# An order and PSUM banks of its own for the first body of an attention loop written as lists of jobs

## The chip, the cores and the metric

One Trainium2 chip, one core of it. The metric is the device time of one execution in microseconds (us), as the median of several runs. The profile is of one further execution, recorded by the hardware profiler. TensorE is called PE, VectorE DVE, ScalarE ACT, GpSimd POOL, and SyncE, which issues the DMAs, SP.

## The reference

A transformer layer on x of 4 x 1024 x 256, all in float32. Layer norm, then attention with 16 heads: queries through a rank of 64, keys and values through a compressed rank of 64, a rotary part of 64 columns, a causal softmax over 1024 tokens, and the output product; then layer norm and a mixture of experts. Both are added to x. What matters here is the attention:

```python
qf = jnp.concatenate([q_nope, _rope(q_pe)], axis=-1)
kf = jnp.concatenate([k_nope, _rope(k_pe)], axis=-1)
scores = jnp.einsum('bhnd,bhmd->bhnm', qf, kf) * scale
scores = jnp.where(causal, scores, jnp.finfo(scores.dtype).min)
attn = jax.nn.softmax(scores, axis=-1)
out = jnp.einsum('bhnm,bhmd->bhnd', attn, v)
x = x + out.transpose(0, 2, 1, 3).reshape(b, n, HEADS * VDIM) @ Wout
```

The kernel has folded the key weights into the queries, so that a query and a key each have 128 numbers (64 of the latent, 64 rotary).

## The kernel before

Three stages follow each other: `attention_prepare` (keys, values and folded weights of all four batches), `attention`, and `ffn` (router and experts).

`attention` works on 32 **pairs of heads** (8 pairs for each of 4 batches). It is software pipelined: a **body** r holds jobs of several pairs, -1 <= r <= 32, and `age` (line 984) says which pair a job of body r belongs to. The jobs, with c the half of the tokens (512 queries), a the head in the pair:

- `Q(c,a)`: PE multiplies out 512 queries of a head, two matmuls of 512 columns. Then DVE does `ROT` (three instructions, lines 1333 and 1335), POOL `ADD` (line 1412), ACT `HIGH` (line 1262, the high part of a split of a float32 in two), POOL `LOW` (line 1419, the rest).
- `S(c,a,j)`: PE makes the scores of query block 4c + j (128 queries) against the (4c + j + 1) x 128 keys that the causal mask leaves: 128 to 512 columns for c = 0, 640 to 1024 for c = 1. Three products (high x high, high x low, low x high), each in one piece of at most 512 columns for c = 0 and in two for c = 1. DVE's `MAX` (line 1321) adds the mask and takes the row's maximum, ACT's `EXP` (line 1270) makes the exponentials in SBUF and their sum.
- `T(c,kb,a)`: PE transposes the 128 x 128 blocks of the exponentials for key block kb (line 1196), up to four, into one of three PSUM banks of their own; `OUT` copies them to SBUF, on ACT (line 1281) or DVE (line 1346). A `T` waits for all four `EXP` of its c and a, and for the `OUT` three transposing jobs back.
- `PV(c,first,n)`: PE multiplies them by the values; `O` on DVE, `OHIGH` on ACT, `OLOW` on POOL follow.
- `INV` (DVE), `REP` (POOL), `L` (PE) and `LOUT` (ACT) invert the sums of the softmax and repeat them; `Y` (PE) and `ACC` (DVE) add the output product to x.

The order of the work is written out by hand, in one list for each engine: `TENSOR`, `VECTOR`, `SCALAR`, `POOL` (lines 924 to 956), with `BANK` giving each `Q`, `S`, `L` and `Y` one of PSUM's banks 0 to 3 (two neighbours for the scores of c = 1). Each engine goes through its list in order, and waits at the head of it on semaphores. One list serves all bodies; a body leaves out the jobs whose pair doesn't exist. So body -1 has only `Q(0,1)` and `Q(0,0)`, the first half's queries of pair 0. Body 0 has all `Q`, all `S`, `L(0)`, the eight `T(0,...)` and `PV(0,0,4)`, and none of the 16 `T(1,...)`, of `PV(1,...)`, `L(1)` and `Y` that stand between the scores in later bodies. A job on banks 0 to 3 waits till the last user of its banks is through: for scores that is their `EXP`, for queries their `ROT` (`bank_users`, line 1039).

The first thing that DVE does in `attention` is to clear a small tile and the mask's 896 left columns (line 1376), and to wait for the DMA that brings the other 128 (line 1377); the first `ROT` is behind these. SP issues the mask's DMA first, then two stores of folded weights and the load of x.

Of the kernel before, what the change touches and what calls it, by code (L numbers as in the profile page):

```python
# [18 lines left out]
P = 128  # L19
# [10 lines left out]
QC = 512  # L30
# [795 lines left out]
def attention(nc, t, ins):  # L826
# [3 lines left out]
    with ExitStack() as ctx:  # L830
# [3 lines left out]
        def sem(name):  # L834
# [126 lines left out]

        def R(part):
# [33 lines left out]

        def body(order, r):

            return [x for x in order if exists(x, r)]

# [5 lines left out]
                for x in order if x[0] == "out"}  # L1008
        LISTS = {"S": SS, "Q": QS, "L": [x for x in TENSOR if x[0] == "l"], "T": TS, "PV": PVS,
                 "Y": [x for x in TENSOR if x[0] == "y"]}  # L1010
        KIND = {"s": "S", "q": "Q", "l": "L", "t": "T", "p": "PV", "y": "Y"}
        COUNT = {}
        for name, xs in LISTS.items():
            done = [(x, r) for r in BODIES for x in body(xs, r)]
            COUNT.update({(name, x, r): n + 1 for n, (x, r) in enumerate(done)})

        def evac(x, r):

            return "scalar" if r == LAST else EVAC[x]

        for engine in ("scalar", "vector"):
            done = [(x, r) for r in BODIES for x in body(TS, r) if evac(x, r) == engine]
            COUNT.update({(engine, x, r): n + 1 for n, (x, r) in enumerate(done)})
# [8 lines left out]

        def slot(x):
            return 512 * BANK[x]

        def banks_of(x):
            return (BANK[x], BANK[x] + 1) if x[0] == "s" and x[1] == 1 else (BANK[x],)

        def bank_users(x, r):

            users = set()
            for bank in banks_of(x):
                order = [y for y in TENSOR if y in BANK and bank in banks_of(y)]
                n, rr = order.index(x), r
                while rr >= -1:
                    n, rr = (n - 1, rr) if n else (len(order) - 1, rr - 1)
                    y = order[n]
                    if exists(y, rr):
                        users.add((y, rr))
                        break  # L1050
            return sorted(users, key=str)
# [78 lines left out]
        def _(pe):  # L1130
            def run(r):
# [16 lines left out]
                def q_job(x):  # L1148
                    _, c, a = x
                    pair = r + age(x)  # L1150
                    batch_loaded(pair)
                    if pair >= 2:
                        pe.wait_ge(wq_loaded[pair % 2], 16 * (pair // 2))
                    banks_free(x)
                    rhs = t.xq[:, pair // PAIRS % 2, c * QC:(c + 1) * QC]
                    for wp in range(2):
                        last = mm(nc, banks[:, BANK[x], :], t.wqs[:, pair % 2, wp, a * P:(a + 1) * P], rhs, wp == 0, wp == 1)
                    last.then_inc(q_ps, 1)

                def s_job(x):  # L1160
# [5 lines left out]
                    w, off = PW[c][j], place(c, j)  # L1166
                    at = slot(x)
                    tok = slice((4 * c + j) * P, (4 * c + j + 1) * P)
# [9 lines left out]
                def l_job(x):  # L1178
                    pe.wait_ge(l_rep, count(x, r))
                    banks_free(x)  # L1180
                    at = slot(x)
# [38 lines left out]
                def y_job(x):  # L1220
# [4 lines left out]
                    for k in range(2):  # L1225
                        tok = slice((4 * c + 2 * i + k) * P, (4 * c + 2 * i + k + 1) * P)
                        out = sps[:, slot(x) + k * D:slot(x) + (k + 1) * D]
                        for n, (o, w) in enumerate(((oh, t.w2h), (oh, t.w2l), (ol, t.w2h))):
                            last = mm(nc, out, o[:, tok], w[:, pr, :], n == 0, n == 2)
# [10 lines left out]
                def mask_job(x):  # L1240
# [5 lines left out]
                       "mask": mask_job}  # L1246
                for x in TENSOR_LAST if r == LAST else body(TENSOR, r):
                    job[x[0]](x)
# [5 lines left out]
        def _(act):  # L1254
            def run(r):
# [8 lines left out]
                def exp_job(x):  # L1264
                    _, c, a, j = x
                    off, w, at = POFF[c][j], PW[c][j], slot(S(c, a, j)) + place(c, j)
                    if r > 0:
# [15 lines left out]
                def lout_job(x):  # L1283
                    _, c = x
                    act.wait_ge(l_ps, count(L(c), r))
                    if exists(L(c), r - 1):
                        act.wait_ge(o_sb, count(L(c), r - 1))
                    nc.scalar.copy(linv_b[:, c, :], sps[:, slot(L(c)):slot(L(c)) + QC]).then_inc(l_sb, 1)

# [14 lines left out]
                job["router"], job["mask"] = router_job, mask_job  # L1304
                for x in SCALAR_LAST if r == LAST else body(SCALAR, r):
                    job[x[0]](x)
# [7 lines left out]
        def _(dve):  # L1314
            def run(r):
                def max_job(x):
                    _, c, a, j = x
                    at = slot(S(c, a, j)) + place(c, j)
                    dve.wait_ge(s_ready, count(S(c, a, j), r))
# [5 lines left out]
                def rot_job(x):  # L1325
                    _, c, a = x
                    cols = slice(c * QC, (c + 1) * QC)
                    at, k = slot(Q(c, a)), QS.index(Q(c, a)) % 2
                    n = count(Q(c, a), r)
# [18 lines left out]
                def inv_job(x):  # L1348
                    _, c = x
                    dve.wait_ge(e_done, count([y for y in SS if y[1] == c][-1], r + age(x)))  # L1350
                    if exists(L(c), r - 1):
# [11 lines left out]
                def acc_job(x):  # L1363
# [6 lines left out]
                    nc.vector.tensor_tensor(acc[:, tiles, :].rearrange("p t d -> p (t d)"),  # L1370
                                            sps[:, slot(Y(c, i)):slot(Y(c, i)) + 2 * D],
                                            acc[:, tiles, :].rearrange("p t d -> p (t d)"), ALU.add).then_inc(y_added, 1)
# [17 lines left out]
                def mask_job(x):  # L1390
# [3 lines left out]
                       "router": router_job, "stats": stats_job, "mask": mask_job}  # L1394
                for x in VECTOR_LAST if r == LAST else body(VECTOR, r):
                    job[x[0]](x)
# [9 lines left out]
        def _(pool):  # L1406
            def run(r):
# [32 lines left out]
                job = {"add": add_job, "low": low_job, "rep": rep_job, "olow": olow_job}  # L1440
                for x in body(POOL, r):
                    job[x[0]](x)
# [448 lines left out]
```

## Time and profile before

| | us |
|---|---|
| median of 3 runs | 1767.05 (1766.79 to 1767.30) |
| the profiled execution, its own time | 1768.51 |
| its span from first to last instruction | 1766.7 |
| `attention_prepare`, to its last matmul | 0 to 69.6 |
| body -1, from its first matmul | 72.4 |
| body 0, from its first scores | 79.64 |
| body 1, from its first scores `S(0,1,0)` | 119.89 |
| body 2, the same | 155.87 |
| busy: PE, DVE, ACT, POOL | 1697.7, 1239.1, 982.4, 571.9 |

The times in the profile are from the start of the span. A busy time of PE holds the time in which a matmul's last columns drain. PEclk is the clock that PE was granted, as a share of 2.4 GHz; its two levels are 1.00 (2.4 GHz) and 0.50 (1.2 GHz).

### The profile page before, as it was taken

The page shows a single profiled execution, that of the slowest core. Times are in us where ns is not written, and L with a number is a line of the kernel's source. Part 1 is how long each engine was busy: PE and PEld are TensorE (multiplying, and loading weights), DVE is VectorE, ACT ScalarE, POOL GpSimd, SP SyncE. Part 2 cuts the span into 40 slices and gives each one's busy share as a digit, 9 for nine tenths or more (in the row PEclk, how much of TensorE's full clock was granted, in tenths as well). Part 3 has the DMA queues.
Part 4 walks back from the last instruction along what each step waited for, and adds up shares of the span by engine and source line. Part 5 has one row for each costly group of instructions (what it writes and reads, how often), then busy time and mean ns, then how long its engine had stood idle before and what let it go on. Part 6 is the DMA issues. An engine that isn't in the chain of part 4 may idle for free. (4 is left out here: it accounts for less than half of the span.)

```text
span 1766.7 us, 32116 instructions
## 1 busy us (share of the span) xinstructions
PE 1697.7 (96%) x11280; PEld 1390.1 (79%) x11280; DVE 1239.1 (70%) x2860; ACT 982.4 (56%) x2316; POOL 571.9 (32%) x497
## 2 busy tenths in 40 slices
PE   5689999999999999999999999999899999999998
PEld 4567777777777777777877777777689999999998
DVE  6778778878788878877878878877555454554543
ACT  6556666666666666666666666665433333333332
POOL 4434334443444333443444334434301110110100
PEclk9889999999999999999999999999999999999999
DMA  8300000002000002000001100000300000000000
GB/s 281 115 13 7 7 7 7 13 7 96 7 13 7 7 7 84 26 7 7 7 13 42 61 7 13 7 7 19 102 1 25 25 1 24 25 1 25 13 13 13
DMA packets 35805, 51.45 MB, mean 29 GB/s; under 512 B 2305, under 2 KB 26881, under 8 KB 35649
## 3 DMA queue, kind: packets, MB, share of 16 engines
q1 hardware_dynamic: 35648, 49.39, 8.5%
q8 instruction: 95, 1.56, 0.4%
q14 instruction: 62, 0.50, 0.1%
HBM read 35.23 MB, written 14.16 MB: 28 GB/s over the span
## 5 line engine op out<-in xcount | busy, mean ns | idle before, releaser
L1270 ACT ACTIVATE probs<-aps,nmax 128x1024 f32<-128x1024 f32 (+7 forms) x512 | 378.9, 745 | 228.4 <-DVE nmax L1321 223.0
L1321 DVE CUSTOM_DVE_ANT_0 aps<-aps,mask_row 128x1024 f32<-128x1024 f32 (+7 forms) x512 | 388.7, 770 | 146.6 <-PE aps L43 141.2
L1196 PE MATMUL aps<-ident,probs 128*128 128x128 f32 x2304 | 330.6, 273 | 0.6 <-ACT pT L1281 0.6
L43 PE MATMUL aps<-kTh,qh 128*128 128x512 f32 (+3 forms) x768 | 296.1, 386 | 14.0 <-POOL ql L1419 7.5
L1196 PEld LDWEIGHTS aps<-ident,probs 128*128 128x128 f32 x2304 | 272.8, 141 | 22.9 <-issue 1.6
L1281 ACT COPY pT<-aps 128x512 f32<-128x512 f32 (+3 forms) x483 | 233.0, 506 | 91.0 <-PE aps L1196 88.5
L43 PE MATMUL aps<-pT,v 128*64 128x512 f32 (+3 forms) x1536 | 268.9, 492 | 0.6 <-ACT pT L1281 0.6
L43 PE MATMUL aps<-kTl,qh 128*128 128x512 f32 (+3 forms) x768 | 259.8, 345 | 0.0
L1412 POOL TENSOR_TENSOR rot<-rot 64x512 f32<-64x512 f32 x128 | 163.9, 1281 | 186.9 <-DVE rot L1335 186.9
L43 PE MATMUL aps<-kTh,ql 128*128 128x512 f32 (+3 forms) x768 | 224.3, 346 | 0.0
L43 PEld LDWEIGHTS aps<-pT,v 128*64 128x64 f32 x1536 | 101.5, 136 | 152.7 <-issue 142.6
L1419 POOL TENSOR_TENSOR ql<-rot,qh 128x512 fp32r<-128x512 f32 x128 | 164.6, 1286 | 139.8 <-ACT qh L1262 139.8
L1437 POOL TENSOR_TENSOR ol<-o,oh 128x512 fp32r<-128x512 f32 x64 | 82.6, 1291 | 363.4 <-ACT oh L1295 363.4
L43 PEld LDWEIGHTS aps<-kTh,qh 128*128 128x128 f32 x768 | 147.0, 191 | 65.7 <-issue 45.0
L1670 ACT CAST aTh<-fps 128x512 fp32r<-128x512 f32 (+1 forms) x96 | 52.8, 551 | 236.7 <-PE fps L1588 236.6
L1727 DVE TENSOR_TENSOR aTl<-fps,aTh 128x512 fp32r<-128x512 f32 (+1 forms) x96 | 62.0, 646 | 166.9 <-ACT aTh L1670 166.9
L43 PE MATMUL fps<-wth,qh 128*128 128x352 f32 x512 | 175.9, 344 | 2.0 <-PEq L830 2.0
L1335 DVE TENSOR_TENSOR rot<-aps,sinT 32x512 f32<-32x512 f32 x256 | 174.2, 680 | 3.5
L43 PE MATMUL fps<-wtl,qh 128*128 128x352 f32 x512 | 165.8, 324 | 0.0
L43 PE MATMUL fps<-wth,ql 128*128 128x352 f32 x512 | 165.6, 323 | 0.0
L43 PEld LDWEIGHTS aps<-kTl,qh 128*128 128x128 f32 x768 | 148.0, 193 | 10.1
L43 PEld LDWEIGHTS aps<-kTh,ql 128*128 128x128 f32 x768 | 137.3, 191 | 8.5
(190 smaller groups left out, 3038.8 us busy)
## 6 DMA issues: line engine op xcount, KB each, us to landing
wqs<-wq_scratch SPq DMA_DIRECT2D x30, 256.0 KB, 2.7
raw_numbers<-in_x SPq DMA_DIRECT2D x4, 1024.0 KB, 7.0
acc<-in_x SPq DMA_DIRECT2D x8, 512.0 KB, 3.6
x_scratch<-acc SPq DMA_DIRECT2D x8, 512.0 KB, 3.0
x<-x_scratch SPq DMA_DIRECT2D x8, 512.0 KB, 3.9
out<-x SPq DMA_DIRECT2D x7, 512.0 KB, 2.9
heads<-in_heads SPq DMA_DIRECT2D x4, 640.0 KB, 9.7
wout<-in_Wout SPq DMA_DIRECT2D x4, 512.0 KB, 9.6
```

The source lines that it names most:

```text
L43: return nc.tensor.matmul(out, lhsT, rhs, start=start, stop=stop, skip_group_check=True)
L1196: last = nc.tensor.transpose(tps[:, TS.index(x) % 3, j * P:(j + 1) * P], probs[c][:, c * (pair % 2), a, off:off + P], t.ident[:])
L1270: nc.scalar.activation(probs[c][:, c * (r % 2), a, off:off + w], sps[:, at:at + w], ACT.Exp, bias=nmax[:, c, a, j:j + 1], scale=-1.0, accu ...
L1281: nc.scalar.copy(pT[:, k % PT_BUFS, s:QC], tps[:, k % 3, s:QC]).then_inc(t_sb["scalar"], 1)
L1321: nc.vector.tensor_tensor_reduce(out=s, in0=s, in1=mask[:, N - PW[c][j]:N], scale=-1.0, scalar=3.0e38, op0=ALU.add, op1=ALU.min, accum_out ...
L1335: last = nc.vector.tensor_tensor(rot2[to:to + 32, k, :], sps[source:source + 32, at:at + QC], t.sinT[to:to + 32, cols], ALU.mult)
L1412: nc.gpsimd.tensor_tensor(rot1[0:64, k, :], rot1[0:64, k, :], rot2[:, k, :], ALU.add).then_inc(q_add, 1)
L1419: nc.gpsimd.tensor_tensor(ql[:, a, cols], rot1[:, k, :], qh[:, a, cols].bitcast(F32), ALU.subtract).then_inc(q_split, 1)
L1437: nc.gpsimd.tensor_tensor(ol[:, cols], o32[:, c, :], oh[:, cols].bitcast(F32), ALU.subtract).then_inc(o_low, 1)
L1670: nc.scalar.copy(aTh[:, i % 2, m.start:m.stop, :].rearrange("p m n -> p (m n)"), turned_in(i, q)[:, 0:len(m) * P]).then_inc(aT_h, 1)
L1727: nc.vector.tensor_tensor(aTl[:, i % 2, m.start:m.stop, :].rearrange("p m n -> p (m n)"), turned_in(i, q)[:, 0:len(m) * P], aTh[:, i % 2, ...
```

## The change

Body 0 gets four lists of its own and a table of banks of its own; all other bodies keep theirs. In body 0 `Q(1,1)` comes first, the scores of head 1 come before those of head 0, `Q(1,0)`, `Q(0,1)` and `Q(0,0)` stand between scores, and the transposes `T(0,...)` are spread from the eleventh scores on. The eight copies `OUT(0,...)` of body 0, of which DVE had six and ACT two, go four to each. The functions that count jobs for the semaphores and find the last user of a bank now take the body into account. And the clearing of the mask moves from DVE to POOL, with a semaphore `mask_cleared`; the two waits for the mask move from ahead of DVE's first `ROT` to its first `MAX`.

```diff
+        TENSOR_FIRST = [Q(1, 1), S(0, 1, 2), S(0, 1, 0), S(0, 1, 1), S(0, 1, 3), S(0, 0, 1), S(0, 0, 0), Q(1, 0),
+                        S(0, 0, 2), S(0, 0, 3), S(1, 1, 1), Q(0, 1), T(0, 1, 0), T(0, 0, 1), S(1, 1, 0), S(1, 1, 2),
+                        T(0, 0, 0), S(1, 0, 0), T(0, 1, 1), Q(0, 0), T(0, 3, 1), T(0, 2, 0), L(0), S(1, 0, 2),
+                        S(1, 0, 3), T(0, 3, 0), T(0, 2, 1), S(1, 1, 3), S(1, 0, 1), PV(0, 0, 4)]
+        VECTOR_FIRST = [ROT(1, 1), MAX(0, 1, 2), MAX(0, 1, 0), MAX(0, 1, 1), MAX(0, 1, 3), MAX(0, 0, 1), MAX(0, 0, 0),
+                        ROT(1, 0), MAX(0, 0, 2), MAX(0, 0, 3), MAX(1, 1, 1), ROT(0, 1), INV(0), OUT(0, 0, 1),
+                        MAX(1, 1, 0), MAX(1, 1, 2), OUT(0, 0, 0), MAX(1, 0, 0), ROT(0, 0), OUT(0, 2, 0), MAX(1, 0, 2),
+                        MAX(1, 0, 3), OUT(0, 2, 1), MAX(1, 1, 3), MAX(1, 0, 1), O(0)]
+        SCALAR_FIRST = [EXP(0, 1, 2), EXP(0, 1, 0), EXP(0, 1, 1), HIGH(1, 1), EXP(0, 1, 3), EXP(0, 0, 1), EXP(0, 0, 0),
+                        EXP(0, 0, 2), HIGH(1, 0), EXP(0, 0, 3), EXP(1, 1, 1), OUT(0, 1, 0), HIGH(0, 1), EXP(1, 1, 0),
+                        EXP(1, 1, 2), OUT(0, 1, 1), EXP(1, 0, 0), OUT(0, 3, 1), LOUT(0), HIGH(0, 0), EXP(1, 0, 2),
+                        OUT(0, 3, 0), EXP(1, 0, 3), EXP(1, 1, 3), EXP(1, 0, 1), OHIGH(0)]
+        POOL_FIRST = [ADD(1, 1), LOW(1, 1), ADD(1, 0), LOW(1, 0), ADD(0, 1), REP(0), LOW(0, 1), ADD(0, 0), LOW(0, 0),
+                      OLOW(0)]
+        BANK_FIRST = {Q(1, 1): 2, S(0, 1, 2): 3, S(0, 1, 0): 1, S(0, 1, 1): 0, S(0, 1, 3): 2, S(0, 0, 1): 3,
+                      S(0, 0, 0): 1, Q(1, 0): 0, S(0, 0, 2): 2, S(0, 0, 3): 3, S(1, 1, 1): 0, Q(0, 1): 2,
+                      S(1, 1, 0): 0, S(1, 1, 2): 2, S(1, 0, 0): 0, Q(0, 0): 2, L(0): 3, S(1, 0, 2): 0, S(1, 0, 3): 2,
+                      S(1, 1, 3): 0, S(1, 0, 1): 2}
+        FIRST_BY_VECTOR = [T(0, 0, 1), T(0, 0, 0), T(0, 2, 0), T(0, 2, 1)]
...
-        def body(order, r):
-
-            return [x for x in order if exists(x, r)]
+        def body(order, first, r):
+
+            return [x for x in (first if r == 0 else order) if exists(x, r)]
...
+            if r == 0:
+                return "vector" if x in FIRST_BY_VECTOR else "scalar"
             return "scalar" if r == LAST else EVAC[x]
...
+        def bank_of(x, r):
+            return (BANK_FIRST if r == 0 else BANK)[x]
...
+        USERS = {bank: [(x, r) for r in BODIES for x in tensor_body(r) if x in BANK and bank in banks_of(x, r)]
+                 for bank in range(4)}
 
         def bank_users(x, r):
...
+            for bank in banks_of(x, r):
+                n = USERS[bank].index((x, r))
+                users.update(USERS[bank][n - 1:n] if n else [])
             return sorted(users, key=str)
...
                 def max_job(x):
                     _, c, a, j = x
-                    at = slot(S(c, a, j)) + place(c, j)
+                    at = slot(S(c, a, j), r) + place(c, j)
+                    if r == 0 and x == next(y for y in VECTOR_FIRST if y[0] == "max"):
+                        dve.wait_ge(mask_loaded, 16)
+                        dve.wait_ge(mask_cleared, 1)
                     dve.wait_ge(s_ready, count(S(c, a, j), r))
...
                     nc.vector.memset(t.spot_v.tensor[:], 0.0)
-                    nc.vector.memset(mask[:, 0:N - P], 0.0)
-                    dve.wait_ge(mask_loaded, 16)
...
+            nc.gpsimd.memset(mask[:, 0:N - P], 0.0).then_inc(mask_cleared, 1)
             nc.gpsimd.memset(ones[:], 1.0)
```

## Rows read from the trace of the kernel before

**Rows 1.** The page's first two parts: busy time, and busy tenths in 40 slices

```profile
PE 1697.7 (96%) x11280; PEld 1390.1 (79%) x11280; DVE 1239.1 (70%) x2860; ACT 982.4 (56%) x2316; POOL 571.9 (32%) x497
...
PE   5689999999999999999999999999899999999998
```

**Rows 2.** Window of body 1, from first scores to first scores: length, engines, clock, DMA

```profile
119.89:155.87 35.98, 35.67 (x236) 27.56 (x234) 28.65 (x61) 23.87 (x57) 14.82 (x13) 1.00 0.04 9
```

**Rows 3.** Windows of PE alone in body 0: length, busy, granted clock, DMA

```profile
79.64:92.35 12.71, 9.12 (x27) 0.50 0.00 0
92.35:99.15 6.80, 3.61 (x17) 1.00 0.15 39
99.15:109.35 10.20, 8.98 (x29) 0.50 0.01 2
109.35:119.89 10.54, 9.16 (x59) 1.00 0.00 0
...
79.64:119.89 40.25, 30.87 (x128) 0.72 0.03 7
```

**Rows 4.** What PE waited for, 70 to 124 us: us, times, longest

```profile
PE aps L43 <- POOL ql L1419: 7.5, 2, 5.2
PE aps L43 <- ACT probs L1270: 3.8, 4, 1.6
```

**Rows 5.** PE in order of time: start, duration, instruction, idle before it

```profile
72.43 2.05 PE L43 MATMUL aps<-xq,wqs 128*128 128x512 f32 x4 [2.87 <-PEq L67]
79.64 0.47 PE L43 MATMUL aps<-kTh,qh 128*128 128x128 f32 x1 [5.17 <-POOL ql L1419]
...
88.89 0.55 PE L43 MATMUL aps<-kTh,qh 128*128 128x256 f32 x1 [0.62 <-DVE rot L1335]
...
89.67 0.63 PE L43 MATMUL aps<-kTh,qh 128*128 128x512 f32 x1
90.10 0.63 PE L43 MATMUL aps<-kTl,qh 128*128 128x512 f32 x1
...
99.85 0.77 PE L43 MATMUL aps<-kTh,qh 128*128 128x512 f32 x1 [1.63 <-ACT probs L1270]
...
107.25 1.06 PE L1196 MATMUL aps<-ident,probs 128*128 128x128 f32 x4
107.96 0.78 PE L43 MATMUL aps<-kTh,qh 128*128 128x512 f32 x1
...
115.26 0.39 PE L43 MATMUL aps<-kTh,qh 128*128 128x512 f32 x1
115.49 0.39 PE L43 MATMUL aps<-kTl,qh 128*128 128x512 f32 x1
...
116.73 2.38 PE L43 MATMUL aps<-pT,v 128*64 128x512 f32 x16
...
119.89 0.30 PE L43 MATMUL aps<-kTh,qh 128*128 128x128 f32 x1
```

**Rows 6.** DVE in order of time, from its first instruction of the stage

```profile
72.71 0.81 DVE L1376 MEMSET mask_row<- 128x896 f32 x1
74.19 0.69 DVE L1333 TENSOR_TENSOR rot<-aps,cosT 128x512 f32<-128x512 f32 x1 [0.67 <-DMA mask_row<-in_mask]
74.89 1.37 DVE L1335 TENSOR_TENSOR rot<-aps,sinT 32x512 f32<-32x512 f32 x2
```

**Rows 7.** POOL in order of time: the chain of a query's parts

```profile
76.34 1.26 POOL L1412 TENSOR_TENSOR rot<-rot 64x512 f32<-64x512 f32 x1 [3.82 <-DVE rot L1335]
78.33 1.26 POOL L1419 TENSOR_TENSOR ql<-rot,qh 128x512 fp32r<-128x512 f32 x1 [0.73 <-ACT qh L1262]
```

**Rows 8.** Groups by shape, 72 to 125 us: busy, mean ns of one | idle before

```profile
L1270 ACT ACTIVATION_READ_ACCUMULATOR probs<-aps,nmax 128x1 f32 x20 | 4.0, 200 | 0.0
...
L1321 DVE CUSTOM_DVE_ANT_0 aps<-aps,mask_row 128x1024 f32<-128x1024 f32 x2 | 2.5, 1232 | 2.2 <-PE aps L43 2.2
...
L1270 ACT ACTIVATE probs<-aps,nmax 128x1024 f32<-128x1024 f32 x2 | 2.2, 1114 | 3.7 <-DVE nmax L1321 3.7
```

More of the change, by code:

```diff
@@ L997, in attention, with tensor_body @@
         BODIES = range(-1, B * PAIRS + 1)
-        def body(order, r):
-            return [x for x in order if exists(x, r)]
+        def body(order, first, r):
+            return [x for x in (first if r == 0 else order) if exists(x, r)]
+        def tensor_body(r):
+            return body(TENSOR, TENSOR_FIRST, r)
         TS = [x for x in TENSOR if x[0] == "t"]
@@ L1031, in out_count, with slot, banks_of @@
             return COUNT[evac(x, r), x, r]
[L1033 to L1037, printed above, removed]
+        def bank_of(x, r):
+            return (BANK_FIRST if r == 0 else BANK)[x]
+        def slot(x, r):
+            return 512 * bank_of(x, r)
+        def banks_of(x, r):
+            return (bank_of(x, r), bank_of(x, r) + 1) if x[0] == "s" and x[1] == 1 else (bank_of(x, r),)
+        USERS = {bank: [(x, r) for r in BODIES for x in tensor_body(r) if x in BANK and bank in banks_of(x, r)]
+                 for bank in range(4)}
         def bank_users(x, r):
             users = set()
[L1042 to L1050, printed above, removed]
+            for bank in banks_of(x, r):
+                n = USERS[bank].index((x, r))
+                users.update(USERS[bank][n - 1:n] if n else [])
             return sorted(users, key=str)
@@ L1156, in q_job @@
                     for wp in range(2):
-                        last = mm(nc, banks[:, BANK[x], :], t.wqs[:, pair % 2, wp, a * P:(a + 1) * P], rhs, wp == 0, wp == 1)
+                        last = mm(nc, banks[:, bank_of(x, r), :], t.wqs[:, pair % 2, wp, a * P:(a + 1) * P], rhs, wp == 0, wp == 1)
                     last.then_inc(q_ps, 1)
@@ L1166, in s_job @@
                     w, off = PW[c][j], place(c, j)
-                    at = slot(x)
+                    at = slot(x, r)
                     tok = slice((4 * c + j) * P, (4 * c + j + 1) * P)
@@ L1180, in l_job @@
                     banks_free(x)
-                    at = slot(x)
+                    at = slot(x, r)
                     for j in range(4):
@@ L1246, in run @@
                        "mask": mask_job}
-                for x in TENSOR_LAST if r == LAST else body(TENSOR, r):
+                for x in TENSOR_LAST if r == LAST else tensor_body(r):
                     job[x[0]](x)
@@ L1265, in exp_job @@
                     _, c, a, j = x
-                    off, w, at = POFF[c][j], PW[c][j], slot(S(c, a, j)) + place(c, j)
+                    off, w, at = POFF[c][j], PW[c][j], slot(S(c, a, j), r) + place(c, j)
                     if r > 0:
@@ L1304, in run @@
                 job["router"], job["mask"] = router_job, mask_job
-                for x in SCALAR_LAST if r == LAST else body(SCALAR, r):
+                for x in SCALAR_LAST if r == LAST else body(SCALAR, SCALAR_FIRST, r):
                     job[x[0]](x)
@@ L1327, in rot_job @@
                     cols = slice(c * QC, (c + 1) * QC)
-                    at, k = slot(Q(c, a)), QS.index(Q(c, a)) % 2
+                    at, k = slot(Q(c, a), r), QS.index(Q(c, a)) % 2
                     n = count(Q(c, a), r)
@@ L1394, in run @@
                        "router": router_job, "stats": stats_job, "mask": mask_job}
-                for x in VECTOR_LAST if r == LAST else body(VECTOR, r):
+                for x in VECTOR_LAST if r == LAST else body(VECTOR, VECTOR_FIRST, r):
                     job[x[0]](x)
@@ L1440, in run @@
                 job = {"add": add_job, "low": low_job, "rep": rep_job, "olow": olow_job}
-                for x in body(POOL, r):
+                for x in body(POOL, POOL_FIRST, r):
                     job[x[0]](x)
```

17 lines of the change are left out of this document (8 added, 9 removed).

## The prediction

> **What bounds the kernel now.** The page first: PE is busy 96% of the span, and its busy tenths are 9 in nearly every slice; only the first slices and the last aren't full [rows 1]. Next, windows cut from one body's first scores to the next one's: body 1 lasts 35.98 us, and PE is busy for 35.67 of them, all at the full clock [rows 2]. The later ones run by the same lists. So a later body has no room: whatever the first body gains moves the rest of the kernel forward by as much. The same window over body 0: 40.25 us, though it lacks 16 of 24 transposing jobs, two of three value products and all output products. PE is busy for only 30.87, and for 22.9 us of it was granted 0.50 of its clock; two stretches hold 9.12 and 8.98 us of matmuls at that level [rows 3]. The waits say why PE stands: 7.5 us in two waits for POOL's low part of the queries (5.2 of them ahead of the very first scores), 3.8 us in four for `EXP` to free a bank [rows 4]. So body 0 is bounded by latencies between the engines and by the clock that they cost, not by PE's work.
>
> **The parts of the change.** First the ones with a short answer.
>
> *Mask.* DVE now does 0.81 us of clearing and 0.67 of waiting for the mask's DMA before its first `ROT`, which starts at 74.19 [rows 6]. Both go from there. PE's four first query matmuls start at 72.43, a slot of 0.43 each at half clock and 0.63 for the last to drain [rows 5], so `Q(0,1)` is ready at about 73.5 and `ROT` starts at 73.6: 0.6 us earlier. Then the chain as now: `ROT` 2.06, `ADD` 1.26, 0.73 till `LOW`, `LOW` 1.26 [rows 6, 7]. First scores at 79.1 instead of 79.64.
>
> POOL's clearing of 896 columns is not in the trace. DVE's takes 0.81 [rows 6]; POOL's two-input instruction on 512 columns takes 1.26 [rows 7], 2.2 for 896. I take 1.6, between the two since neither is near. POOL is free from 72.5 and has its first `ADD` at 75.8, so up to 3.3 us are covered, and the first `MAX` (81.2) is later still. It costs nothing at either bound; beyond 3.3 each us would delay the queries by one. The mask's DMA has landed by 74.19, 7 us before that `MAX`. Two waits more in front of one `MAX` cost no time then. No DMA moves on SP's queue, though the load of pair 2's weights, which waits for the last `Q(1,.)` of body 0, is issued some 9 us earlier.
>
> *Copies.* Two of the eight `OUT(0,...)` move from DVE to ACT. Both engines have idle time in body 0, so only the place in the order counts, which the walk below holds.
>
> *Order and banks.* This is the sum, and I walk the new lists through with the durations of the trace, each engine in its order, each job starting at the later of its engine and its waits. A 512-column matmul takes a slot of 0.43 at half clock and 0.23 at full; four transposes 0.71, and half of that at full; the first value product 2.3 [rows 5]. Narrower ones in proportion, not under half of a 512 one. On 1024 columns `MAX` takes 1.29 and `EXP` 1.2, both with the read of their accumulator [rows 8]; on fewer in proportion, over a fixed 0.2 for `MAX` and 0.3 for `EXP`. Between engines I add 0.03 to 0.15, as the rows' gaps have it.
>
> I tried the walk on the old lists first, with the clock's two returns where rows 3 have them: it puts body 1's first scores at 120.06, and the row says 119.89 [rows 5]. Then the new lists (starts in us; in brackets what a wait of over 0.15 was for):
>
> | PE job | start | PE job | start |
> |---|---|---|---|
> | `Q(0,1) Q(0,0) Q(1,1)` | 72.43 | `T(0,0,0)` | 93.2 |
> | `S(0,1,2)` | 79.1 (`LOW(0,1)`) | `S(1,0,0)` | 94.6 (`EXP(1,1,0)`, 1.0) |
> | the six scores to `S(0,0,0)` end | 84.0 | `Q(0,0)` | 96.0 |
> | `Q(1,0)` | 84.0 | `L(0)` | 96.9 |
> | `S(0,0,2) S(0,0,3)` | 85.0 | `S(1,0,2)` | 97.8 (`EXP(1,0,0)`, 0.6) |
> | `S(1,1,1)` | 87.4 (`ROT(1,0)`, 0.8) | `S(1,0,3)` | 99.1 |
> | `Q(0,1)` | 88.7 (`EXP(0,0,2)`, 0.2) | `S(1,1,3)` | 101.9 (`EXP(1,0,2)`, 1.1) |
> | `T(0,1,0)` | 90.1 (`EXP(0,0,3)`, 0.8) | `S(1,0,1)` | 103.4 |
> | `S(1,1,0)` | 91.0 (`EXP(1,1,1)`, 0.2) | `PV(0,0,4)` | 104.5 to 106.8 |
> | `S(1,1,2)` | 91.9 | `S(0,1,0)` of body 1 | 108.0 |
>
> What sets it: `LOW(0,0)` ends at 82.3, before `S(0,0,1)` needs it, so the second of the two waits for POOL is gone. `Q(1,1)` is made at 74.2, and POOL works on it right behind `LOW(0,0)`: `LOW(1,1)` ends at 85.5, before `S(1,1,1)`; now that chain starts only at 86.7. Behind `PV`, body 1's first transposes wait 0.4 us for `EXP(1,0,1)`, ended at 107.1. On DVE `ROT(1,1)` is put ahead of the first `MAX` and itself waits for `LOW(0,1)` (79.1) to free its buffer; it holds DVE till 81.2 while four scores pile up in four banks. PE has work all the same, since by 82.7 the first `EXP` has freed a bank.
>
> By parts: the start 0.55; `Q(1,1)` in a time in which PE stood, 0.5 at full clock; PE's standing inside the body from about 11 us in the walk of the old lists (9.4 in the row, 40.25 less 30.87, where a draining matmul counts as busy) to 5.2, so 5.8; matmuls at half clock from 18.1 us to 6.3, each us of which holds 0.45 that the full clock would save, 5.3. Together 12.1; the walk itself gives 119.9 - 108.0 = **11.9 us**, which I take.
>
> **The clock** is the part that rows don't give. Before, it came back at 92.35, 3.4 us after PE's last stop, at 88.89, and at 109.35, 9.5 us after it had taken up work at 99.85 and with 8.98 us of matmuls in the 10.20 before; it fell at 99.15, after 3.61 us of matmuls in 6.80 [rows 3, 5]. In the walk PE works without a gap from 79.1 to 84.9, so I put the return at 85.5, between 82.5 and 88.6, the 3.4 and the 9.5 us from 79.1. By those ends body 1's first scores start at 107.1 or 108.8, a gain of 12.8 or 11.1. After that PE's longest wait is 1.1 us and it works some 80% of the time, against 53% before the fall, so I let it stay. The Trainium skill speaks against that: "TensorE: Matmul & The Clock Gate", section "A second HAM failure mode: psum-queue depth-cycling", describes a kernel whose many short stops between groups of matmuls, each waiting for a PSUM bank, make the clock go up and down. By that rule the forecast would lose what the rival below prices.
>
> **The sum.** The profiled execution took 1768.5, its span 1766.7 and 1.8 around it; less 11.9 that is 1756.6. The median of the runs shown is 1767.05, 1.5 below it, and 11.9 from it gives **1755.2**. For these 1.5 us there is no row; a body 0 in which the clock came back once and stayed would, by the walk of the old lists, be 2.7 shorter. If the timed runs are like that, the gain is only 9.2, and the time 1757.8.
>
> **The rivals.**
>
> *The clock comes back late or falls again* (0.15). For: eleven short waits in the body, and in the old body 0 the return at 109.35 took 9.5 us of dense work. Against: none of the new waits is over 1.1 us between 79.1 and 107. With the return at 99.15 instead of 85.5 the walk puts body 1's first scores at 111.1: a gain of 8.8, **1758.2**. It is the mechanism that the page's rule above names.
>
> *Half clock through the whole body* (0.03): the walk gives 117.2, a gain of 2.7, 1764.4, which is no change that can be told. Against: even the old, thinner order got the clock back twice.
>
> *Slower* (0.03): the same mechanism, but past the body. If the clock hasn't come back when body 1 starts at 117.2, every us of dense work at half clock costs 0.45. From 123.2 on that eats the 2.7, from 131 it is over 0.2% slower. Held through body 1, which then lasts some 65 us for 36, it would cost 29 less 2.7: about **1793**. Against: from 109.35 on the clock stayed full through the end of body 0 and body 1 [rows 2, 3], and body 1's lists don't change.
>
> *The gain is given back* (0.04): the change does shorten body 0, but PE then waits at a later point that doesn't move, say for a DMA: 1767. For it, only that pair 2's weights and x come from memory. Against: SP issues them on PE's own progress, and in body 1 PE stands for 0.3 us [rows 2].
>
> **How the numbers follow.** The forecast, a gain of 11.1 to 12.8, has 0.75: 1754.2 to 1756. The range must hold the late clock (1758.2), timed runs with a shorter body 0 (1757.8), and at the low end a clock back still sooner or durations some per cent shorter over 29 us: 1753.6 to 1758.8. A measurement of this kernel can tell some 0.2% (3.5 us) from no change. Faster by more: 0.93. Within: half clock, most of given back, 0.04. Slower: 0.03.
>
> **What would show it.** In the profile after: DVE's first `ROT` at 73.6 with no memset before it; a POOL memset of 896 columns that ends before 75.8; first scores (128x384) at 79.1; one wait for POOL's low part, not two; all PE waits after it under 1.2 us, most for `EXP`; granted clock 1.00 from between 82 and 89 and no second fall; body 1's first 128-column scores at 107 to 109; bodies 1 and 2 at 36.0. Wrong would be: a clock of 0.50 past 90, a wait of over 2 us for a low part (`S(1,1,1)` or `S(1,0,0)`), or a body 1 longer than 36.2.

## The result and the profile after

The changed kernel takes 1757.61 us (median of 4 runs, 1757.32 to 1757.68) against 1767.14 for the kernel before (4 runs), a ratio of 0.9946 with a 95% interval of 0.9929 to 0.9963. That is 9.5 us faster; the forecast was 11.9 (1755.2), the range 1753.6 to 1758.8. Timed again in five rounds it took 1758.01 beside 1767.73: 0.9946 (0.9932 to 0.9959), 9.7 us.

The profiled execution of the changed kernel took 1757.32 with a span of 1755.5. Against the profiled execution of before its span is 11.2 us shorter, more than the medians say; that gap is taken up below.

The page's first two parts, for [rows 1]:

```profile
PE 1692.5 (96%) x11280; PEld 1384.9 (79%) x11280; DVE 1237.4 (70%) x2857; ACT 983.1 (56%) x2318; POOL 573.4 (33%) x498
...
PE   5799999999999999999999999999899999999998
```

Windows of PE alone (length, busy, granted clock, DMA): body 0 from its first scores to the clock's return, from there to body 1's first scores, and both together, for [rows 3]; then body 1 with all engines, for [rows 2]:

```profile
79.92:84.60 4.68, 4.68 (x17) 0.50 0.08 28
84.60:108.13 23.53, 19.94 (x111) 1.00 0.04 12
79.92:108.13 28.21, 24.62 (x126) 0.92 0.05 15
...
108.13:144.12 35.99, 35.69 (x235) 27.56 (x234) 28.23 (x60) 23.81 (x57) 14.79 (x13) 1.00 0.03 8
```

Body 0 takes 28.2 us for 40.25, and PE stands for 3.6 of them for 9.4. It works at half clock for 4.7 us for 18.1, then at the full clock to the end of body 1. Body 1 is what it was, 35.99 for 35.98. What PE waited for, 70 to 112 us, for [rows 4] (us, times, longest):

```profile
PE aps L43 <- POOL ql L1445: 3.9, 1, 3.9
PE aps L43 <- PEq L67: 2.9, 1, 2.9
PE aps L43 <- ACT probs L1295: 2.4, 4, 0.9
PE aps L1221 <- ACT probs L1295: 0.6, 1, 0.6
PE aps L43 <- issue: 0.4, 1, 0.4
```

One wait for a low part is left, the one ahead of the very first scores. PE in order of time, for [rows 5]: the queries with `Q(1,1)` among them, the first scores, `S(1,0,0)` behind its wait, `S(1,1,3)` behind the longest one, the value product, and body 1's first scores:

```profile
73.72 2.27 PE L43 MATMUL aps<-xq,wqs 128*128 128x512 f32 x6 [2.88 <-PEq L67]
79.92 0.69 PE L43 MATMUL aps<-kTh,qh 128*128 128x384 f32 x1 [3.92 <-POOL ql L1445]
...
94.93 0.41 PE L43 MATMUL aps<-kTh,qh 128*128 128x384 f32 x1 [0.78 <-ACT probs L1295]
...
102.15 0.47 PE L43 MATMUL aps<-kTh,qh 128*128 128x512 f32 x1 [0.91 <-ACT probs L1295]
...
104.84 2.37 PE L43 MATMUL aps<-pT,v 128*64 128x512 f32 x16
107.28 1.09 PE L1221 MATMUL aps<-ident,probs 128*128 128x128 f32 x8
108.13 0.30 PE L43 MATMUL aps<-kTh,qh 128*128 128x128 f32 x1
```

And the start on POOL and DVE, for [rows 6] and [rows 7]: POOL's clearing, DVE's first `ROT`, POOL's first `ADD`, DVE's `ROT(1,1)` and its first `MAX`:

```profile
73.68 0.85 POOL L1488 MEMSET mask_row<- 128x896 f32 x1 [0.67 <-POOLq L67]
...
76.62 1.26 POOL L1438 TENSOR_TENSOR rot<-rot 64x512 f32<-64x512 f32 x1 [2.01 <-DVE rot L1363]
```

```profile
74.46 0.69 DVE L1361 TENSOR_TENSOR rot<-aps,cosT 128x512 f32<-128x512 f32 x1 [0.59 <-PE aps L43]
...
79.97 0.69 DVE L1361 TENSOR_TENSOR rot<-aps,cosT 128x512 f32<-128x512 f32 x1 [1.32 <-POOL ql L1445]
80.67 1.37 DVE L1363 TENSOR_TENSOR rot<-aps,sinT 32x512 f32<-32x512 f32 x2
82.08 0.57 DVE L1349 CUSTOM_DVE_ANT_0 aps<-aps,mask_row 128x384 f32<-128x384 f32 x1
```

The stage before `attention`, which the change doesn't touch, ends later in this trace: the first query matmul is at 73.72, not 72.43. So the stretch to compare is from there to body 1's first scores: 34.41 us, where the walk had 35.6 (108.0 - 72.4) and the trace of before has 47.46 (119.89 - 72.43). Of these 13.0 us 1.3 go in the longer first stage.

### The profile page after: what moved, and what is told of

Read it like the earlier page. It is cut to its first block and busy times, and to the rows that moved or that the text cites. A ratio compares the mean times of both kernels' runs of the same rounds, so it can differ in the third digit from the quotient of the medians.

```text
span 1755.5 us, 32117 instructions
## 1 busy us (share of the span) xinstructions
PE 1692.5 (96%) x11280; PEld 1384.9 (79%) x11280; DVE 1237.4 (70%) x2857; ACT 983.1 (56%) x2318; POOL 573.4 (33%) x498
## 5 line engine op out<-in xcount | busy, mean ns | idle before, releaser
L1295 ACT ACTIVATE probs<-aps,nmax 128x384 f32<-128x384 f32 (+7 forms) x512 | 379.0, 745 | 219.3 <-DVE nmax L1349 213.8
L1349 DVE CUSTOM_DVE_ANT_0 aps<-aps,mask_row 128x384 f32<-128x384 f32 (+7 forms) x512 | 388.7, 770 | 134.6 <-PE aps L43 129.1
```

The costliest lines, as they stand in the source:

```text
L1295: nc.scalar.activation(probs[c][:, c * (r % 2), a, off:off + w], sps[:, at:at + w], ACT.Exp, bias=nmax[:, c, a, j:j + 1], scale=-1.0, accu ...
L1349: nc.vector.tensor_tensor_reduce(out=s, in0=s, in1=mask[:, N - PW[c][j]:N], scale=-1.0, scalar=3.0e38, op0=ALU.add, op1=ALU.min, accum_out ...
```

## The experiments

Twelve runs of eleven kernels, the two known ones among them. Each was timed beside the kernel before; the gain is against that kernel's median in the same set of runs (1766.78 to 1767.73). The "stretch" is what was just defined, read from each profile. Where a kernel was timed, the 95% interval of its ratio is 1.6 to 3 us to either side, so smaller differences between variants are read from the stretches and not from the medians.

| kernel | first query matmul | stretch | median us | gain |
|---|---|---|---|---|
| before, first profile | 72.43 | 47.46 | 1767.14 | |
| before, again | 73.24 | 44.28 | 1766.17 (one run) | |
| changed | 73.72 | 34.41 | 1757.61 | 9.5 |
| changed, again | 73.94 | 34.63 | 1757.91 (one run) | |
| changed, five rounds | 74.30 | 34.57 | 1758.01 | 9.7 |
| mask's part alone | 73.75 | 43.61 | 1765.92 | 0.9 |
| lists alone | 73.95 | 35.15 | 1757.62 | 9.2 |
| before, PE kept at work | 73.99 | 41.78 | 1764.49 | 2.5 |
| changed, PE kept at work | 73.23 | 34.27 | 1757.68 | 9.4 |
| queries late | 74.16 | 38.25 | 1761.88 | 5.2 |
| copies six and two | 73.74 | 35.22 | 1757.72 | 9.3 |
| heads by turns | 73.33 | 39.26 | 1761.12 | 5.9 |
| `ROT(1,1)` later | 72.78 | 38.39 | 1761.16 | 5.9 |
| more banks | 73.89 | 32.95 | 1755.57 | 11.5 |

**The same kernels again.** The theory was the walk's: the order decides, and the instants at which the clock returns are a second matter that differs from one execution to the next. The rival: the two first profiles are typical. Both kernels ran unchanged.

> The kernel before, unchanged, for a second profile. Theory A (the instants at which PE's clock returns differ from one execution to the next, and that moves this kernel): body 1's first scores at another time than 119.89, between 116 and 121, and PE's clock returns and falls at other times; where the first stage's clock comes back later, the first stage ends up to 1.3 us later. Theory B (the profiled execution of before is typical): 119.9 within 0.3, clock returns at 92.3 and 109.4 as before, time 1768.5.

> The changed kernel, unchanged, for a second profile. Theory A: body 1's first scores start 34.4 us (within 1) after body -1's first matmul whatever the clock's instants, since PE works densely enough for one early return; the first stage ends between 69.5 and 70.9. Theory B: everything as in the first profile, 108.1 and 1757.3.

The kernel before, windows of PE alone between the changes of its clock, and then its waits, 70 to 118 us:

```profile
73.24:80.38 7.14, 1.70 (x5) 0.53 0.72 232
80.38:87.40 7.02, 4.69 (x14) 0.51 0.00 0
87.40:90.60 3.20, 1.57 (x9) 1.00 0.00 0
90.60:94.10 3.50, 3.50 (x10) 0.52 0.00 0
94.10:100.80 6.70, 3.45 (x15) 1.00 0.15 39
100.80:104.40 3.60, 3.60 (x13) 0.53 0.00 0
104.40:117.50 13.10, 11.20 (x72) 1.00 0.01 1
```

```profile
PE aps L43 <- POOL ql L1419: 7.7, 2, 5.4
PE aps L43 <- ACT probs L1270: 3.8, 4, 1.6
...
PE aps L1183 <- POOL lrep L1428: 1.6, 1, 1.6
```

The waits are those of [rows 4]; the clock isn't that of [rows 3]. It came back three times and fell twice in between, PE worked at half clock for 11.8 us after its first scores (4.69, 3.50 and 3.60) for 18.1, and the stretch was 3.2 us shorter. The changed kernel's three stretches lie within 0.25 us. So the profile of before that the forecast was made against held a clock worse than its next one, and the theory stands. (One bound of the second expectation was missed: the first stage's last matmul ended at 71.07, past the 70.9 named.) The fall at 90.6 came behind two short stops, with 1.57 us of matmuls in the 3.20 before it:

```profile
88.02 0.36 PE L43 MATMUL aps<-kTh,qh 128*128 128x256 f32 x1 [0.66 <-ACT probs L1270]
...
89.63 0.35 PE L43 MATMUL aps<-kTh,qh 128*128 128x256 f32 x1 [1.01 <-DVE rot L1335]
```

The timed runs settle how typical the first profile was, since each has its mean granted clock on record. Of the 51 runs of the kernel before that were timed beside the variants, 13 had a mean of 0.989 or 0.990 and took 1767.79 to 1769.01 us; the other 38 had 0.991 to 0.995 and took 1764.66 to 1767.96, with a median of 1766.7. The profiled execution of before had 0.989 and took 1768.51: only three of the 51 took longer. The second profile had 0.992.

The first stage shows the same at another place. In the first profile of before its matmuls of 512 columns take slots of 0.2 us from 20.5 on, in that of the changed kernel only from 23.2 on (read from the slots: the granted clock in the profile's rows is 1.00 throughout this stage):

```profile
20.54 0.69 PE L43 MATMUL wps<-xTh,w_in 128*128 128x512 f32 x2
21.07 0.40 PE L43 MATMUL wps<-xTl,w_in 128*128 128x512 f32 x1
```

```profile
21.54 0.63 PE L43 MATMUL wps<-xTl,w_in 128*128 128x512 f32 x1
21.96 1.05 PE L43 MATMUL wps<-xTh,w_in 128*128 128x512 f32 x2
22.82 0.60 PE L43 MATMUL wps<-xTl,w_in 128*128 128x512 f32 x1
23.24 0.64 PE L43 MATMUL wps<-xTh,w_in 128*128 128x512 f32 x2
```

That is 1.1 of the 1.3 us by which its first stage ends later; the rest was there before these matmuls. The first query matmul, which follows that stage, starts anywhere from 72.4 to 74.3 in the table, and 72.43 is the earliest.

**The change's two halves.** First the mask's part in the kernel before:

```diff
+        mask_cleared = sem("mask_cleared")
...
+                    if r == 0 and x == next(y for y in VECTOR if y[0] == "max"):
+                        dve.wait_ge(mask_loaded, 16)
+                        dve.wait_ge(mask_cleared, 1)
...
-                    nc.vector.memset(mask[:, 0:N - P], 0.0)
-                    dve.wait_ge(mask_loaded, 16)
...
+            nc.gpsimd.memset(mask[:, 0:N - P], 0.0).then_inc(mask_cleared, 1)
```

> Only the mask's part of the change: POOL clears it, DVE's first ROT doesn't wait. The forecast's term says 0.55 us from the first scores, and the walk of the old lists, over the instants at which the clock may return, 0.2 to 0.7 us at body 1's first scores: 1766.5 (1766.3 to 1767). Rival: the start matters through the clock, and the gain or loss is over 1.5 us.

Then the lists alone: the changed kernel with the clearing on DVE again, and its wait for the mask's DMA ahead of the first `ROT`:

```diff
-                    if r == 0 and x == next(y for y in VECTOR_FIRST if y[0] == "max"):
-                        dve.wait_ge(mask_loaded, 16)
-                        dve.wait_ge(mask_cleared, 1)
...
+                    nc.vector.memset(mask[:, 0:N - P], 0.0)
+                    dve.wait_ge(mask_loaded, 16)
...
-            nc.gpsimd.memset(mask[:, 0:N - P], 0.0).then_inc(mask_cleared, 1)
```

> The new lists and banks, with the mask cleared by DVE and waited for ahead of the first ROT as in the kernel before. The walk puts body 1's first scores 0.3 to 0.6 us later than with the whole change: 1758.1 (1757.8 to 1758.7), so nearly all of the gain. Rival: the mask's move was needed for the early return of the clock; then 1759 or more.

1765.92 (ratio 0.9994, 0.9985 to 1.0003) and 1757.62 (0.9947, 0.9935 to 0.9959). Both lie a little under the ranges expected (1766.3 and 1757.8 at the low end), by less than their own intervals. The mask's part alone can't be told from no change. Its stretch of 43.61 is the third for the old order, with the clock back once, at 95.1, and kept. In the lists' body it is worth 0.6 us of stretch, 35.15 against 34.57, which the medians don't resolve either. The gain is the lists'. The rival that the mask's move was needed for the early clock is out: without it the clock still came back at 85.5 and stayed.

**The clock by itself.** In the old lists PE does transposes of the identity into bank 7, which nothing uses yet, wherever it stood:

```diff
+        FILLS = {S(0, 1, 0): 27, S(0, 0, 0): 14, S(0, 0, 1): 3, S(0, 1, 1): 4, S(1, 1, 2): 5, L(0): 12, S(1, 0, 3): 12,
+                 S(1, 1, 0): 5, S(1, 1, 1): 8}
...
+                def fill(n):
+                    for k in range(n):
+                        nc.tensor.transpose(banks[:, 7, 0:P], t.ident[:], t.ident[:])
...
                 for x in TENSOR_LAST if r == LAST else body(TENSOR, r):
+                    if r == 0:
+                        fill(FILLS.get(x, 0))
                     job[x[0]](x)
```

> The old lists; in body 0 PE also does transposes of the identity into bank 7 (unused till the value product) where it would stand: 27 ahead of the first scores, 3 to 14 ahead of eight later jobs. The output is unchanged. Theory (the clock is a term of its own): granted clock back by 82 and kept, body 1's first scores 42 to 43.5 us after the first query matmul instead of 44.9 (44.2 to 47.5 seen), time 2 to 4 us under the kernel before: 1763.8 (1762.8 to 1765). PE's standing for the low parts and EXP stays. Rival (the order alone is the gain, the clock follows it for nothing): within 0.7 of the kernel before, or slower by the transposes that come in the way.

1764.49 (0.9984, 0.9975 to 0.9993): 2.5 us gained by more work. The granted clock was 1.00 from 78.4 on, and came back while PE did transposes alone. These 27, and then the longest of the remaining stops of PE, in order of time:

```profile
75.01 4.78 PE L1237 MATMUL aps<-ident 128*128 128x128 f32 x27
81.26 0.33 PE L43 MATMUL aps<-kTh,qh 128*128 128x128 f32 x1 [1.48 <-POOL ql L1428]
84.48 0.33 PE L43 MATMUL aps<-kTh,qh 128*128 128x128 f32 x1 [1.11 <-POOL ql L1428]
...
103.20 0.41 PE L43 MATMUL aps<-kTh,qh 128*128 128x384 f32 x1 [1.01 <-ACT probs L1279]
```

The first scores still start 7.3 us behind the first query matmul and the second ones 3.2 behind those: the chain over DVE, ACT and POOL has its own length, whatever PE's clock. The full clock shortens the stretch to 41.8, a little under the 42 to 43.5 expected. So the clock alone is worth 2.5 us in the old order, net of what the transposes cost. One of the 51 plain runs of the kernel before had a mean granted clock of 0.995, and took 1764.66.

In the changed kernel, 20 transposes ahead of the first scores:

```diff
+        FILLS = {S(0, 1, 2): 20}
```

> The changed kernel with 20 transposes of the identity into bank 7 ahead of the first scores, where PE stands 4 us for the low part. The output is unchanged. Theory: the clock comes back up to 3.4 us sooner, the scores of head 1 run at the full clock, 0.3 to 1.2 us gained: 1756.8 (1756.3 to 1757.4). Rival: the scores then only wait for MAX and EXP, which ROT(1,1) holds up till 82, and nothing is gained.

1757.68 (0.9948, 0.9935 to 0.9960), 0.1 from the changed kernel's: the rival holds. Timed in the same set as the old lists with PE kept at work, this is 6.8 us under them, with the clock back early and kept in both (stretches 34.27 and 41.78). That is what the change is worth with the clock taken out. The clock was back by 77 and the scores of head 1 ran at the full clock, but then PE stood:

```profile
79.75 0.45 PE L43 MATMUL aps<-kTh,qh 128*128 128x384 f32 x1 [1.10 <-POOL ql L1453]
...
82.02 0.47 PE L43 MATMUL aps<-kTh,qh 128*128 128x512 f32 x1 [0.79 <-DVE rot L1371]
...
83.43 0.35 PE L43 MATMUL aps<-kTh,qh 128*128 128x256 f32 x1 [0.47 <-ACT probs L1303]
```

`S(0,1,3)` waits for `ROT(1,1)` to free `Q(1,1)`'s bank, the next ones for `EXP`. In the new order the first scores wait on DVE's and ACT's jobs, and a faster PE gains nothing.

**The order's parts**, undone one at a time in the changed kernel. The queries:

```diff
-        TENSOR_FIRST = [Q(1, 1), S(0, 1, 2), S(0, 1, 0), S(0, 1, 1), S(0, 1, 3), S(0, 0, 1), S(0, 0, 0), Q(1, 0),
-                        S(0, 0, 2), S(0, 0, 3), S(1, 1, 1), Q(0, 1), T(0, 1, 0), T(0, 0, 1), S(1, 1, 0), S(1, 1, 2),
+        TENSOR_FIRST = [S(0, 1, 2), S(0, 1, 0), S(0, 1, 1), S(0, 1, 3), S(0, 0, 1), S(0, 0, 0), Q(1, 1),
+                        S(0, 0, 2), S(0, 0, 3), Q(1, 0), S(1, 1, 1), Q(0, 1), T(0, 1, 0), T(0, 0, 1), S(1, 1, 0), S(1, 1, 2),
```

with `ROT`, `HIGH` and the two banks to match.

> The changed kernel with Q(1,1) and Q(1,0), their ROT and HIGH, put back behind the scores of c = 0, about where the old list has them (Q(1,1) seventh, Q(1,0) tenth). The walk puts body 1's first scores 3.3 to 3.9 us later: 1761.2 (1760.6 to 1762), with PE standing 3 us or more for LOW(1,1) ahead of S(1,1,1). Rival (what counts is the dense start by heads, which stays): under 1 us lost.

1761.88, a gain of 5.2 for 9.6: 4.4 us lost (9.6 is the mean of the changed kernel's two). PE's wait for POOL's low part is there a second time, 3.7 us ahead of 91.60. The clock fell 0.8 us behind it (0.50 from 92.4 to 95.8), with 3.40 us of matmuls at that level:

```profile
PE aps L43 <- POOL ql L1445: 8.7, 2, 5.0
```

The heads' order:

```diff
-        TENSOR_FIRST = [Q(1, 1), S(0, 1, 2), S(0, 1, 0), S(0, 1, 1), S(0, 1, 3), S(0, 0, 1), S(0, 0, 0), Q(1, 0),
-                        S(0, 0, 2), S(0, 0, 3), S(1, 1, 1), Q(0, 1), T(0, 1, 0), T(0, 0, 1), S(1, 1, 0), S(1, 1, 2),
+        TENSOR_FIRST = [Q(1, 1), S(0, 1, 2), S(0, 0, 2), S(0, 1, 0), S(0, 0, 0), Q(1, 0), S(0, 1, 1), S(0, 0, 1),
+                        S(0, 1, 3), S(0, 0, 3), S(1, 1, 1), Q(0, 1), T(0, 1, 0), T(0, 0, 1), S(1, 1, 0), S(1, 1, 2),
```

with `MAX`, `EXP` and the banks to match.

> The changed kernel with the scores of c = 0 by turns from head 1 and head 0, as the old list has them, and banks to fit; the rest as changed, the early queries too. Second scores then wait for LOW(0,0). The walk puts body 1's first scores 2.9 us later: 1760.5 (1759.5 to 1761.5), with two waits of PE for POOL's low part instead of one. Rival (only when the queries are made matters): under 1 us lost.

1761.12, 3.7 us lost. The two waits for a low part were named; the longer waits for `EXP`, 4.9 us for 2.4, were not, and behind the longest of them the clock fell once more (0.50 from 90.6 to 94.1):

```profile
PE aps L43 <- POOL ql L1445: 5.7, 2, 3.8
PE aps L43 <- ACT probs L1295: 4.9, 5, 2.0
```

The place of one job on DVE:

```diff
-        VECTOR_FIRST = [ROT(1, 1), MAX(0, 1, 2), MAX(0, 1, 0), MAX(0, 1, 1), MAX(0, 1, 3), MAX(0, 0, 1), MAX(0, 0, 0),
+        VECTOR_FIRST = [MAX(0, 1, 2), MAX(0, 1, 0), MAX(0, 1, 1), ROT(1, 1), MAX(0, 1, 3), MAX(0, 0, 1), MAX(0, 0, 0),
```

> The changed kernel with ROT(1,1) fourth on DVE, behind three MAX, instead of first, where it holds up the first MAX by 0.8 us. The walk puts body 1's first scores 2.9 us later (4.0 with a later clock): Q(1,1)'s bank is kept till ROT(1,1) is through, and S(0,1,3) waits 2.8 us for it: 1760.5 (1760 to 1761.8). Rival (ROT ahead of MAX is a cost): 0.3 to 0.8 us gained.

1761.16, 3.7 us lost, and PE waited 2.7 us for `ROT` ahead of `S(0,1,3)`, whose bank `Q(1,1)` held. Holding up three `MAX` is the cheaper evil. The clock has a part in the loss that isn't told apart: in this profile it came back at 76.1, fell at 79.5, and came back to stay at 89.7, 16.9 us behind the first query matmul, where the changed kernel's three have 10.9 to 11.4.

```profile
PE aps L43 <- DVE rot L1363: 2.7, 1, 2.7
```

In these last three the intervals of the ratios are wide (0.9952 to 0.9983 over the three, for 0.9932 to 0.9959 of the changed kernel in five rounds), but the slowest run of the changed kernel took 1758.85 and the shortest of theirs 1760.42.

The copies:

```diff
-        FIRST_BY_VECTOR = [T(0, 0, 1), T(0, 0, 0), T(0, 2, 0), T(0, 2, 1)]
+        FIRST_BY_VECTOR = [T(0, 1, 0), T(0, 0, 1), T(0, 1, 1), T(0, 2, 0), T(0, 3, 0), T(0, 2, 1)]
```

with the `OUT` jobs in the two lists to match.

> The changed kernel with the eight copies of body 0 dealt out as in the old lists: six on DVE, two on ACT. The walk puts body 1's first scores 0.5 us later: 1758.1 (1757.7 to 1758.6). Rival (the sharing is a main part of the gain, since DVE is the engine that MAX waits for): over 1.5 us lost.

1757.72 (0.9947, 0.9934 to 0.9961). The stretch grew by 0.65 us, as the walk said, but the medians show no difference from the changed kernel. The sharing is at most a small part of the gain.

**A version that beats both.** Most of PE's stops were for `EXP` to free a bank, while banks 4 to 7 stood empty till the first `T` and `PV`:

```diff
-        sps = banks[:, 0:4, :].rearrange("p b n -> p (b n)")
+        sps = banks[:, 0:8, :].rearrange("p b n -> p (b n)")
...
-        TENSOR_FIRST = [Q(1, 1), S(0, 1, 2), S(0, 1, 0), S(0, 1, 1), S(0, 1, 3), S(0, 0, 1), S(0, 0, 0), Q(1, 0),
-                        S(0, 0, 2), S(0, 0, 3), S(1, 1, 1), Q(0, 1), T(0, 1, 0), T(0, 0, 1), S(1, 1, 0), S(1, 1, 2),
+        TENSOR_FIRST = [Q(1, 1), Q(1, 0), S(0, 1, 2), S(0, 1, 0), S(0, 1, 1), S(0, 1, 3), S(0, 0, 1), S(0, 0, 0),
+                        S(0, 0, 2), S(0, 0, 3), S(1, 1, 1), Q(0, 1), T(0, 1, 0), S(1, 1, 0), S(1, 1, 2), T(0, 0, 1),
...
+        BANK_FIRST = {Q(1, 1): 7, S(0, 1, 2): 1, S(0, 1, 0): 4, S(0, 1, 1): 5, S(0, 1, 3): 3, S(0, 0, 1): 2, S(0, 0, 0): 7, Q(1, 0): 0,
+                        S(0, 0, 2): 4, S(0, 0, 3): 5, S(1, 1, 1): 0, Q(0, 1): 3, S(1, 1, 0): 0, S(1, 1, 2): 2, S(1, 0, 0): 0, Q(0, 0): 2,
...
-                 for bank in range(4)}
+                 for bank in range(8)}
```

and the later jobs of the four lists moved by a few places.

> A version meant to beat the changed kernel. In body 0 the transposes' three banks and the value product's bank stand empty till the first T and PV: scores of c = 0 and Q(1,1) go there (banks 4, 5, 7), Q(1,0) is made right behind Q(1,1), and the four lists are laid out anew by the same walk. The walk puts body 1's first scores at 105.8 for 108.0, whatever the clock: 1755.6 (1755.1 to 1756.4). Theory (PE now stands for EXP freeing a bank, 2 to 3 us in all): as that. Rival (DVE's work bounds the first 12 us, more banks only move the wait): within 0.5 of the changed kernel, 1757.1 to 1758.1.

1755.57 (0.9933, 0.9920 to 0.9945): 11.5 us under the kernel before, 1.9 more than the changed kernel's 9.6. What PE waited for, 70 to 112 us:

```profile
PE aps L43 <- DVE rot L1362: 3.1, 1, 3.1
...
PE aps L43 <- ACT probs L1294: 1.8, 4, 0.6
PE aps L1220 <- ACT probs L1294: 0.9, 1, 0.9
```

Its slowest run took 1756.20, the shortest of the changed kernel's nine timed ones 1757.32, though the intervals of the two ratios overlap. That it is faster is seen; why is only in part. The waits for `EXP` are 2.7 us for 3.0, so freeing banks took away little of PE's standing. `Q(1,0)` now runs ahead of the first scores, at 78.88, where PE would stand for the low part anyway (the 3.1 us are its own wait ahead of that), and not between scores, where its two matmuls took 0.5 us and `S(1,1,1)`, which by the walk waits for its `ROT`, stood another 0.4. The banks, the place of `Q(1,0)` and the new lists weren't tried one by one.

Last, the changed kernel timed again:

> The changed kernel once more, timed in five rounds beside the kernel before. Theory (the gain of the medians, 9.5, is the typical one, and the 11.2 between the two first profiles holds an unlucky clock of the kernel before): 9.0 to 9.9 us under the kernel before. Rival (the gain depends on the chip or the day): outside 8.5 to 10.5.

9.7 us, with a stretch of 34.57: inside the 9.0 to 9.9 expected.

## Why the prediction was right, and where it was off

*What bounds it, and that a gain in body 0 is a gain of the whole:* right. Bodies 1 are alike, 35.98 and 35.99 us. Of the 11.8 us between the two traces at body 1's first scores 11.2 are left at the end of the span.

*The mask:* the first `ROT` starts 0.74 us behind the first query matmul for 1.76 before; the first scores 6.20 for 7.21. That is 1.0 us where 0.55 was said. The rest is the clock: it fell at 74.4 only, behind the first query matmuls, and not ahead of them. In the variant with `ROT(1,1)` later it fell at 72.5, ahead of them, and the first scores came after 6.68 us; the prediction's numbers give 6.67 (79.1 - 72.43). In the time of the whole it can't be told. POOL's clearing took 0.85 us for an estimate of 1.6 between 0.81 and 2.2: near DVE's price, and covered, as said, by 2 us of standing.

*The order:* the walk put body 1's first scores at 108.0, and the trace has 108.13, but from a start 1.3 us later. From the first query matmul the walk has 35.6 and the traces 34.4 to 34.6: 1.0 us too much, of which the clock's return (11 us behind the start, not 13) and the earlier first scores are the visible parts. The waits it named are there: `EXP(1,1,0)` 0.8 for 1.0, `EXP(1,0,2)` 0.9 for 1.1, one low part, nothing over 1 us after it. PE's standing fell from 9.4 to 3.6 us, by the 5.8 that the prediction said. As differences between kernels the walk did about as well as for the time: it gave 3.3 to 3.9, 2.9, 2.9, 0.5 and -2.2 us for five variants, and the stretches moved by 3.7, 4.7, 3.8, 0.65 and -1.6; the gains by 4.4, 3.7, 3.7, 0.3 and -1.9. The signs and the order of size are right; the stretches are off by up to 1.8 us (heads by turns), the gains by up to 1.1.

*The clock:* right that it comes back once, early, and stays; it was back at 84.6 for 85.5. The Trainium skill's rule on stops between groups of matmuls ("TensorE: Matmul & The Clock Gate", "A second HAM failure mode: psum-queue depth-cycling") doesn't take hold in the new order: six stops of 0.3 to 0.9 us lie behind 84.6 in body 0, and the granted clock is 1.00 to its end. In the old order the traces do show a clock that goes up and down between short stops: it fell at 99.15 in the first profile, where the longest stop since its return was 1.5 us and another had begun, and at 90.6 in the second, behind stops of 0.66 and 1.01. With the mask's part alone it stayed at 1.00 through stops of 1.4, 1.6 and 1.6 us (from 95.1 on). So no size of stop here parts a clock that stays from one that falls. In the variants of the new order it fell again behind stops of 2.0 us (heads by turns), 3.7 (queries late) and 3.8 (`ROT(1,1)` later, ahead of the first scores), not behind shorter ones. Part 1 of that page of the Trainium skill says that the point at which the clock returns varies from run to run; the repeated profiles agree, and show what it is worth here: 3.2 us in one kernel's stretch, and up to 1.9 us in the end of the first stage, which is the same in all these kernels.

*The sum:* here it was off, 11.9 for 9.5. The step that failed is the one that took 119.9, the profiled execution's own start of body 1, as the base, and gave matmuls at half clock 5.3 us of the 12.1. In the next profile of the same kernel they were 11.8 us and not 18.1, and its body 1 began 2.4 us sooner. With PE kept at work throughout, the clock alone was worth 2.5 us. The prediction had this case ("if the timed runs are like that, the gain is only 9.2, and the time 1757.8") and put it in the range, not in the forecast. The 1.5 us between profile and median that it had no row for were the sign of it. Counted from the second profile, PE's standing fell from 9.1 to 3.6 us and its matmuls at half clock from 11.8 to 4.7, which at 0.45 each is 3.2 us for the 5.3 said; the stretches differ by 9.7, close to the medians' 9.5 and 9.7. There is luck in how near the forecast came. The walk's 1.0 us too much for the new lists hid part of the base's error: the two first traces differ by 13.0 in the stretch, not by 11.9. And the measured 1757.6 lies outside 1754.2 to 1756, to which the prediction gave 0.75; it came in where the range had been widened for a shorter body 0. Its chances also leave 0.03 without a reason: 0.75 and 0.15 make 0.90 for a gain that can be told, and it said 0.93.

*The rivals:* the clock came back early and stayed, body 1 took as long as before, and 0.6 of 11.8 us were given back, not all. What a late low part costs, the variants show: with a second wait for one, and the clock falling again behind it or later, the gain was 4.4 and 3.7 us smaller. The two aren't told apart there.

What stays open: how the clock's instants are spread over many executions, since timed runs have only its mean on record; and what the 0.6 us are that go between body 1 and the end, of which 0.3 go in one stop of PE right behind body 2's first scores.

## What to carry to other kernels

A software pipeline's one order is laid out for its full bodies; its first body has other gaps, and a list of its own is cheap where each microsecond moves the whole kernel. Lay it out by the longest chain over the slow engines (here rotate, add, split, subtract, 5.3 us for each query): start those chains in PE's gaps, and work on the half that is ready. Where an engine's clock depends on how it has been used, take the base from several profiles, and compare the profiled execution's own time and mean granted clock with those of the timed runs. A walk of the lists from a trace's durations told the better order from the worse in each variant here, within 1 to 2 us.

## What the runs showed of the hardware

Two profiles of one kernel, with the same waits, differed by 3.2 us in one stage, because the granted clock rose and fell at other instants; over 51 timed runs of that kernel the mean granted clock went from 0.989 to 0.995, and the time from 1769.0 to 1764.7. In that kernel the clock fell behind stops of PE of 0.66 and 1.01 us; in the changed one it stayed at 1.00 through six stops of 0.3 to 0.9, and in the old order with the mask's part alone through three of 1.4 to 1.6. Transposes of an identity, with nothing else on PE from 75.2 on, were enough for the clock to come back at 78.4. This work, which computes nothing, made a kernel 2.5 us faster, in the old order, and no faster that could be measured in the new one, where the first scores waited on other engines. POOL cleared 128 x 896 words in 0.85 us, next to DVE's 0.81, while its two-input instruction takes 1.26 us for 512.
